# A graph network's group transform, carried over two triples of the next group

## The reference

```python
for l in range(3):
    xr = jnp.einsum('nd,rde->rne', x, W_rel[l])        # 8 matrices of 256 x 256
    msg = xr[edge_type, src]
    agg = jax.ops.segment_sum(msg, dst, num_segments=6250)
    x = jax.nn.relu(agg + x @ W_root[l] + bias[l])
# per row m, output n: sign(sign(x) @ sign(w).T) * (|x| @ |w|.T), scaled by the maxima, + bias
```

## Time and profile before

| | |
|---|---|
| median of 3 runs | 7883.08 us (7858.49 to 7887.33) |
| the profiled execution | 7882.25 us, span 7880.5 us |
| PE, matmuls | 4793.6 us, 61% |
| GpSimd (POOL) | 4449.8 us, 56% |
| VectorE (DVE) | 1830.2 us, 23% |
| ScalarE (ACT) | 623.5 us, 8% |
| TensorE clock granted, mean | 0.767 |
| DMA | 672.35 MB, 85 GB/s |

### The profile page before, as it was taken

How to read it: one execution, slowest core, us unless ns; L and a number is a source line. 1 busy time by engine, 2 the same in 40 slices (tenths; PEclk the granted TensorE clock), 3 DMA queues, 4 the chain that set the end, 5 groups by cost and what they waited for, 6 DMA issues and landing times. The chain is left out here.

```text
span 7880.5 us, 83226 instructions
## 1 busy us (share of the span) xinstructions
PE 4793.6 (61%) x26040; PEld 4215.5 (53%) x26041; DVE 1830.2 (23%) x3533; ACT 623.5 (8%) x848; POOL 4449.8 (56%) x4715
## 2 busy tenths in 40 slices
PE   4666666666666566666666666645555555555555
PEld 3555555555555455655565555545454445454454
DVE  3211222212212122222222212222222222222222
ACT  2000000000000000000000000000000000000000
POOL 5555565555655466666666656465555555555553
PEclk7777777777777777777777777777787777777777
DMA  5222232222322222322233322232222222222221
GB/s 168 82 84 85 81 89 85 83 82 83 91 80 81 82 87 88 90 87 88 86 89 89 89 86 87 72 99 78 79 80 78 83 83 78 83 80 78 81 77 58
DMA packets 284193, 672.35 MB, mean 85 GB/s; under 512 B 79916, under 2 KB 133905, under 8 KB 284082
## 3 DMA queue, kind: packets, MB, share of 16 engines
q0 software_dynamic: 225072, 614.90, 26.7%
q1 hardware_dynamic: 30308, 30.00, 1.2%
q10 hardware_dynamic: 28702, 26.46, 1.0%
HBM read 645.36 MB, written 25.68 MB: 85 GB/s over the span
## 5 line engine op out<-in xcount | busy, mean ns | idle before, releaser
L373 POOL DMA_INDIRECT rows<-node_table,idx x4689 | 4442.5, 947 | 3356.7 <-PE bank L389 1415.6
L389 PE MATMUL bank<-onehot,rows 128*128 128x128 f32 x18792 | 2761.7, 304 | 1034.2 <-issue 741.8
L389 PEld LDWEIGHTS bank<-onehot,rows 128*128 128x128 f32 x18792 | 2602.8, 218 | 1193.5 <-issue 1157.9
L470 PE MATMUL bank<-wrel,agg 128*128 128x256 f32 x5568 | 1616.9, 461 | 1574.9 <-DVE agg L928 965.8
L470 PEld LDWEIGHTS bank<-wrel,agg 128*128 128x128 f32 x5568 | 1310.0, 239 | 1847.0 <-issue 1604.9
L915 DVE TENSOR_TENSOR agg<-bank,agg 128x256 f32 x1566 | 663.8, 424 | 4161.3 <-remote 2315.4
L836 DVE TENSOR_TENSOR onehot<-bank,key 128x1152 f32<-128x1152 f32 x525 | 707.4, 1348 | 14.4 <-issue 12.4
L638 ACT COPY agg<-zero_col 128x2304 f32<-128x2304 f32 x174 | 367.3, 2111 | 4211.9 <-PE bank L470 3587.0
L937 DVE SCALAR_TENSOR_TENSOR acc<-bank,in_first,acc 128x256 f32 x174 | 84.1, 484 | 1710.7 <-PE bank L470 939.7
L533 PE MATMUL bank<-ident_bf,sgn 128*128 128x128 bf16 x98 | 18.2, 289 | 393.7 <-DVE mag L975 357.5
L533 PEld LDWEIGHTS bank<-ident_bf,sgn 128*128 128x128 bf16 x98 | 6.7, 104 | 402.9 <-issue 402.9
(11 more groups left out here) (137 smaller groups left out, 790.1 us busy)
## 6 DMA issues: line engine op xcount, KB each, us to landing
rows<-node_table,idx POOLq DMA_INDIRECT x4689
node_table<-new_x ACTq DMA_DIRECT2D x98, 128.0 KB
x_tile<-node_table SPq DMA_DIRECT2D x58, 128.0 KB
x_in<-in_x_dram SPq DMA_DIRECT2D x8, 768.0 KB, 10.8
wrel<-in_L_gnn_W_rel_dram SPq DMA_DIRECT2D x6, 1024.0 KB
xres<-in_x_dram ACTq DMA_DIRECT2D x48, 128.0 KB
out_dram<-res ACTq DMA_DIRECT2D x48, 128.0 KB
node_table<-x_in SPq DMA_DIRECT2D x7, 768.0 KB, 8.1
```

What stands on the lines that cost most here:

```text
L373: pool.indirect_dma_start(rows[:, s:s + D], None, tables[layer % 2], bass.IndirectOffsetOnAxis(ap=idx[:, g * TPG + k, j:j + 1], axis=0),). ...
L389: last = nc.tensor.matmul(to[:, h, :], of[:, s:s + P], hot[:, hot_k * CH + j, :], start=(j == 0), stop=(j == CH - 1))
L470: last = nc.tensor.matmul(out_ps, agg[:, h, r, 0:P], wrel[:, h, r * D:(r + 1) * D], start=(r == 0 and h == 0), stop=(r == R - 1 and h == K ...
```

## The change

PE no longer does a group's transform at the group's end. It becomes a function that runs when the register `owed` is 1, and is called after k1 of the next group, with the count of groups that must be done; it is called too where a loop ends, and ahead of the extra products. The first call finds nothing owed. So that the counts fit, `agg_ready` and `group_done` start one higher, and every wait on `group_done` is raised by one. PE's `turn_ended` moves from behind k3 to behind k4, its `multiply_ended` from behind k6 to behind k7, and VectorE's `result` from behind k7 to behind k8, which is ahead of the fold.

```diff
@@ products that a spread group needs
                 with pe.If(more > 0):
+                    transform(layer, g + layer * GROUPS)
+                    pe.reg_mov(owed, 0)
                     for k in range(TPG):
                         rows_of(layer, g, k)
@@
+            def transform(layer, count):
+
+                with pe.If(pe.snap(owed, min_val=0, max_val=1) > 0):
+                    pe.wait_ge(rel_loaded, 32 * (layer + 1))
+                    pe.wait_ge(agg_ready, count + 1)
+                    pe.wait_ge(group_done, count + 1)
+                    pe.sem_inc(pe_mark, 1)
+                    for r in range(R):
+                        for h in range(KH):
+                            last = nc.tensor.matmul(out_ps, agg[:, h, r, 0:P], wrel[:, h, r * D:(r + 1) * D],
+                                                    start=(r == 0 and h == 0), stop=(r == R - 1 and h == KH - 1))
+                    last.then_inc(out_ready, 1)
@@ PE's group
                     products(seg[k % 3], rows, onehot[:, k // BATCH, :, :], k, k % BATCH).then_inc(seg_ready, 1)
-                    if late and k == TPG // 3:
+                    if k == 1:
+
+                        transform(layer, gg)
+                        pe.reg_mov(owed, 1)
+                    if late and k == TPG // 2:
                         with pe.If(g < late[0]):
                             turn_ended(layer, late[1])
-                    if late and k == TPG - 3:
+                    if late and k == TPG - 2:
                         with pe.If(g < late[0]):
                             multiply_ended(layer, late[1])
@@ end of PE's group
-                pe.wait_ge(rel_loaded, 32 * (layer + 1))
-                pe.wait_ge(agg_ready, gg + 1)
-                pe.wait_ge(group_done, gg + 1)
-                pe.sem_inc(pe_mark, 1)
-                for r in range(R):
-                    for h in range(KH):
-                        last = nc.tensor.matmul(out_ps, agg[:, h, r, 0:P], wrel[:, h, r * D:(r + 1) * D],
-                                                start=(r == 0 and h == 0), stop=(r == R - 1 and h == KH - 1))
-                last.then_inc(out_ready, 1)
@@ PE's loop over tiles, where a tile has no group of its own, and behind the loop
+                        transform(layer, end + layer * GROUPS)
+                        pe.reg_mov(owed, 0)
                         turn_ended(layer, t - 1)
                         multiply_ended(layer, t - 1)
                     pe.sem_inc(pe_mark, 1)
+                transform(layer, (layer + 1) * GROUPS)
+                pe.reg_mov(owed, 0)
                 turn_ended(layer, TILES - 1)
@@ VectorE
-            dve.sem_inc(group_done, 1)
+            dve.sem_inc(group_done, 2)
+            dve.sem_inc(agg_ready, 1)
@@ VectorE's group
-                    if late and k == TPG - 2:
+                    if late and k == TPG - 1:
                         with dve.If(g < late[0]):
                             result(late[1])
@@
-                dve.wait_ge(group_done, gg + 1)
+                dve.wait_ge(group_done, gg + 2)
```

More of the change, by code:

```diff
@@ L382, in _ @@
             pe.reg_mov(extras, 0)
+            owed = pe.alloc_register("pe_owed")
+            pe.reg_mov(owed, 0)
             def products(to, of, hot, k=0, hot_k=0):
@@ L685, in finish_sums @@
                 done = t + layer * TILES
-                act.wait_ge(group_done, end + (layer * GROUPS + 1))
+                act.wait_ge(group_done, end + (layer * GROUPS + 2))
                 act.wait_ge(stored, done * 16 + 16)
@@ L920, in group @@
                             if k == 0:
-                                dve.wait_ge(group_done, late[0] + layer * GROUPS)
+                                dve.wait_ge(group_done, late[0] + (layer * GROUPS + 1))
                             (normalise, magnitudes, scaled)[k](late[1])
-                    if late and k == TPG - 2:
+                    if late and k == TPG - 1:
                         with dve.If(g < late[0]):
@@ L1010, in _ @@
                 with dve.Else():
-                    dve.wait_ge(group_done, end + ((L - 1) * GROUPS + 1))
+                    dve.wait_ge(group_done, end + ((L - 1) * GROUPS + 2))
                     dve.sem_inc(dve_mark, 1)
@@ L1014, in _ @@
                 dve.sem_inc(dve_mark, 1)
-            dve.wait_ge(group_done, L * GROUPS + 1)
+            dve.wait_ge(group_done, L * GROUPS + 2)
             tile_end(TILES - 1)
```

## The result

The kernel after takes 7259.69 us, the median of 4 runs (7244.77 to 7265.74), against 7885.2 us for the kernel before in 4 runs (7858.49 to 7895.22). The profiled execution of the kernel after took 7265.74 us, its span 7264.0 us.

A forecast was written before the change was run, and what follows sets the result against it. GpSimd's gathers, 33.8 us a group, plus its stops for late PE were taken to bound the kernel. Terms -376 + 63 + 63 = -250 us took 7882 to 7632 us, 3.2% faster; range 7410 to 8070 us.

The forecast's parts named there:

- The floor and the stops: GpSimd: 27 gathers take 33.8 us a group; stops waiting for PE to free slots add 11.3 us.
- How far it gets ahead isn't counted as a gain, since all 9 slots bind again nine triples later.: GpSimd: six gathers, 7.5 us, released before the transform instead of behind it; counted as no gain.
- rival 3: Much faster: six gathers under the transform shorten GpSimd's long stall, 479 us, 7153 us; half gives 7392 us; chance 7%.
- The seam: PE between k8 and transform: k0 and k1 cover the 2.2 us wait in 171 groups, -376 us.
- 3 to 10 us: Sign in the profile after: the transform starts this long after k8's add, product matmuls directly before it.
- The new wait: PE before k3, behind the transform: 1.65 us waiting for k0's add; a third, 0.55 us, in 114 groups, +63 us.
- Layer 2: Tile's end delays k0's and k1's adds; lost cover costs 1.1 us in 57 groups, +63 us.
- the moved steps: Transposes, multiply and VectorE's result one triple later: taken as 0; 62 us in layer 2 if uncovered.
- Rival 1: No change: each product costs its bare 1.34 us, the chain grows by 29 us, 7911 us; chance 15%.
- Rival 2: Slower: PE's wait moves from under gathers to where GpSimd stands still, +183 us, 8065 us; chance 25%.

The follow-up runs named there:

- f1: Kernel after, but GpSimd's gathers for k0 and k1 held back until the transform two groups back has ended; 7976.84 us, 0.987 of the kernel before.
- g1: Kernel after itself, unchanged, timed again in the last session, where the kernel before took 6012.6 us; 6018.28 us, 1.0009.
- e3: Kernel before with VectorE's third onehot behind the fold, shortening the seam by 1.35 us; 7761.32 us, 0.986.
- e7: Kernel after without gathers beyond each layer's first group, multiplying old rows; 4809.61 us, 0.596 of the kernel before.
- e11: Kernel after with ScalarE zeroing 16 columns of agg instead of 2304; 7358.79 us, 0.912 of the kernel before.
- e1: Kernel before with only the three moved steps (transposes behind k4, multiply behind k7, result behind k8); 7964.54 us, 1.010.
- e2: Kernel after with the three moved steps put back where they were; 7518.83 us, 0.955 of the kernel before.
- e6: Kernel before without gathers beyond each layer's first group, multiplying old rows; 4875.65 us, 0.604.
- e12: Kernel before with each gather replaced by a direct load of 128 consecutive rows, issued by SyncE; 4828.84 us, 0.598.
- f4: Kernel before with each gather replaced by a direct load of 128 consecutive rows, issued by GpSimd; 4834.24 us, 0.599.
- e8: Kernel before with gathers of 256 bytes a row instead of 1024, as many and as scattered; 8074.92 us, 1.000.
- e5: Kernel after with the transform behind k2 of the next group instead of k1; 7937.3 us, 0.983 of the kernel before.
- f2: Kernel after with VectorE's third onehot behind the fold; 7330.35 us, 0.908 of the kernel before.
- f3: Kernel after with VectorE's three tile-end steps behind k0, k3 and k4, and the transposes behind k5; 7288.97 us, 0.903 of the kernel before.

## Why the prediction was half right

**The floor and the stops: right.** 33.8 us of gathers a group plus GpSimd's stops is what sets the period, and what late products cost is read off there. The idle time of one engine accounts for the gain within 4 us.

**The step that failed: "How far it gets ahead isn't counted as a gain, since all 9 slots bind again nine triples later."** They do bind again: GpSimd still stops in every group. But what the stops cost in all depends on how many gathers it may issue during the transform, the longest stretch in which PE frees no slot. Before, the nine slots ran out with much of the transform still to come, and GpSimd stood through the rest and through k0 behind it. Now six more gathers, 7.5 us, may lie beside it, and the stops fall from 11.3 to 7.9 us a group by the page's waits, where the prediction had 9.9. f1 takes just this release away and 6.6 of the 7.9% go. It is rival 3, given 7%, and its whole price was about right: it put the restart at 2.8 us a group, 479 us; f1 against the kernel after is 0.987 - 0.921 = 0.066, some 520 us of 7885, across two sessions. I believed half of it at most, and added it to a sum of -250 us, of which only about 100 were there (below).

Why it was missed can be seen in the earlier trace rows: one group, in layer 1, with a stop of 5.43 us. In the table above layer 1 has the least to win, 1.0 us a group; layers 0 and 2 have 4.1 and 5.4. A second row of the timeline, from layer 0, where the same stop is longer:

```profile
758.25 0.94 POOL L373 DMA_INDIRECT rows<-node_table,idx  x1 [8.98 <-PE bank L389]
...
849.80 0.94 POOL L373 DMA_INDIRECT rows<-node_table,idx  x1 [9.57 <-PE bank L389]
```

**The seam, -376 us: too large.** The seam didn't close. From k8's add to the transform the median is 2.6 us in layers 0 and 1 and 3.9 in layer 2, with 0.6 us or less between the fold's end and the transform; "3 to 10 us" was wrong in layers 0 and 1, because k0 and k1 are out before k8's late result is. (In g1, where no result is late, it is 5.8 to 7.0 us.) And a microsecond of it is worth 0.46 (e3), not 1: 2.2 x 0.46 x 171 = 173 us would be an estimate by that rate. All that PE's new order gives without the release is 1.3% of 7885, 103 us (f1).

**The new wait, +63 us: right in place, right in size only where results aren't late.** In g1 and e7, layers 0 and 1, k3 starts a median of 3.0 us behind the transform's end and PE waits 1.69 us for it: the 3.0 and 1.65 us that were worked out. In the kernel after the transform's own result is late, k3 starts a median of 9 us behind the recorded end, and the wait is 3.9 us in layer 0 and 7.8 in layer 1. GpSimd has a stop of 1.9 to 2.3 us a group at k3. No run shows what this costs in time: e11, meant for it, left k0's add where it was.

**Layer 2, +63 us, and the moved steps at 0: wrong in sign for the whole.** The layer won most, 5.5 us a group. The steps cost 1% in the old order (e1), against a bound of 62 us, and save 3.4% in the new (e2), a gain that I hadn't looked for: I had asked what moving them costs and not what leaving them costs once k0 and k1 are gone from behind the transform.

**Rival 1, no change, and the rule behind it.** Its working said that the bare chain grows by 29 us; without gathers it shrinks by 66 us, 1.4% (e6, e7). It had both of its parts wrong: layers 0 and 1, which should have won 0.5 us a group, stayed the same and lost 0.4, and layer 2, which should have lost, won 1.6. Why layer 2 wins was not tested. The Trainium skill (SBUF — State Buffer, Who interferes with whom) says that "DMA never contends with a compute engine". For direct loads e12 and f4 agree with it, 0.598 and 0.599, where e6 has 0.604 without any. For GpSimd's indirect gathers the traces of five sessions disagree (adds 5.0 us apart; by e8, 1.000, whatever their bytes), and the last one's agree. There rival 1's result, no change, is what was measured, but by another mechanism: GpSimd's 33.8 us are the floor, and PE is never late.

**Rival 2, slower: not seen.** In e5 a wait that moves out of the gathers may be what takes the gain back, but even there the kernel isn't slower than before (0.983).

**Open.** Why PE's results are late beside indirect gathers in some sessions and not in another, on one chip; whether it goes with the gather's form or with its scattered rows; whether it is the result or only its signal that is late (the record of the products ends early in either case, but ends are modelled); and whether f2 and f3 are better than the kernel after.

## What to carry to other kernels

Where a queue of slots is refilled by an engine that is the floor, ask what it does during the longest step of the engine that empties them: put the first slots' work ahead of that step, so that refilling goes on beside it, and no further, or the wait behind it grows. Look at the refilling engine's stops by slot and by layer, over all groups, before one group's row is taken as typical. And time a kernel in more than one session before a gain of its order of work is believed: here the same two kernels are 7.9% apart or equal.

## What was not expected of the hardware

- 128 rows a time, the same bytes: by GpSimd's indirect gather of scattered rows PE's product idle is 1034.2 us in a kernel of 7882 us (8068 to 8084 us in the sessions of the runs that follow); by a direct load from GpSimd's own queue 139.0 us and 4834 us; from SyncE 4829 us; without loads 4876 us.
- A quarter of the bytes in each indirect gather changes nothing (1.000): the gather takes GpSimd 946 ns instead of 947, and PE's idle time in front of products is 1009.3 us instead of 1034.2.
- Two loads of a group's places by VectorE's sequencer, 0.84 and 0.75 us, hide a zeroing of 2.11 us: with the zeroing at 0.20 us the first add comes no sooner.
- The lateness of PE's results beside these gathers isn't a constant of the chip: 0.13 us in one session, 6.1 us in another for the same instructions, with the gathers at 948 and 949 ns. On chip 7 both levels came within a quarter of an hour. The granted clock was 0.887 there and 0.799 here, and PE idled less; which follows from which the runs don't tell, but at 33.8 us a group PE's clock is not what sets the time.
